# A two-layer kernel whose attention is set up inside the phase before it, and whose first tile's relus all run on one engine

## The reference, cut to what matters

```python
q = jnp.einsum('bnc,ac->bna', X, Wq)          # X is h; a = 64
k = jnp.einsum('bnc,ac->bna', X, Wk)
Vy = jnp.einsum('bnc,dc->bnd', X, Wy_w) + Wy_b
e = jax.nn.relu(_rho_signed_sqrt(q[:, :, None, :] + k[:, None, :, :]))
scores = jnp.einsum('bija,a->bij', e, Wphi)
ex = jnp.exp(scores - jnp.max(scores, axis=-1, keepdims=True))
denom = jnp.sum(ex, axis=-1)
part1 = jnp.einsum('bij,bjc->bic', ex, Vy)
Ew = jnp.einsum('bij,bija->bia', ex, e)
part2 = jnp.einsum('bia,ca->bic', Ew, We_w) + We_b * denom[..., None]
return (part1 + part2) / (denom[..., None] + EPS_DEN)
```

## Time and profile before

| | |
|---|---|
| median of 3 runs | 5102.75 us |
| the profiled execution | 5103.16 us |
| its span, first to last instruction | 5101.5 us |
| busy in the span: PE / DVE / ACT / POOL | 87% / 79% / 67% / 62% |
| phase C's first instruction (SP) to the first root | 1219.28 to 1247.91 us |
| first spread of exponentials in phase C | 1280.37 us |
| last spread | 4377.4 us |

### The profile page before, as it was taken

The page is one execution under the profiler, slowest core; times in us unless marked ns, Lnnn a source line. Parts: engine busy times, 40 slices in busy tenths (PEclk is TensorE's granted clock), DMA queues, the critical chain, the costliest instruction groups (busy, mean ns, idle before and its releaser), DMA issues.

```text
span 5101.5 us, 83954 instructions
## 1 busy us (share of the span) xinstructions
PE 4445.5 (87%) x28586; PEld 2309.7 (45%) x28586; DVE 4020.8 (79%) x6587; ACT 3426.3 (67%) x2401; POOL 3184.0 (62%) x2730
## 2 busy tenths in 40 slices
PE   7888877786889988988988988998898888899998
PEld 4333333464333433433443443443443343577777
DVE  2789895534899999999999999999999999422225
ACT  2232222213999999999999999999988889444343
POOL 0666672433777777777777777777777777243334
PEclk8888887898999999999999999999999999899999
DMA  6000001342000000000000000000000000200002
GB/s 226 0 0 1 0 1 63 116 165 99 1 4 2 2 4 2 17 4 2 2 4 2 17 4 2 2 4 2 11 3 5 2 2 4 100 17 8 16 25 83
DMA packets 70509, 131.01 MB, mean 26 GB/s; under 512 B 8263, under 2 KB 46631, under 8 KB 65888
## 3 DMA queue, kind: packets, MB, share of 16 engines
q1 hardware_dynamic: 61152, 106.21, 6.1%
q0 software_dynamic: 9216, 23.17, 1.2%
HBM read 74.66 MB, written 61.03 MB: 27 GB/s over the span
## 4 chain that ended last, share of the span: by engine, by line
PE 33%; issue 21%; DVE 16%; ACT 13%; POOL 1%; DVEq 1%; DMA 1%; ACTq 0%; POOLq 0%; SPq 0%
PE banks L2206 11%; ACT e_slots L615 10%; PE banks L518 8%; DVE e_slots L858 7%; PE banks L477 7%; DVE e_slots L813 2%; DVE ew L858 1%; PE banks L1641 1%; ACT L632 1%; ACT e_slots L606 1%; PE banks L490 1%; PE banks L292 1%; PE banks L1695 1%; PE banks L1704 1%; PE banks L1592 1%
## 5 line engine op out<-in xcount | busy, mean ns | idle before, releaser
L858 DVE CUSTOM_DVE_ANT_0 e_slots<-e_slots,banks 128x1024 f32<-128x1024 f32 x2048 | 2444.9, 1216 | 120.1 <-PE banks L518 103.6
L615 ACT ACTIVATE e_slots<-e_slots 128x4096 f32<-128x4096 f32 x512 | 1841.1, 3620 | 75.7 <-DVE e_slots L813 51.1
L518 PE MATMUL banks<-ex_parts,sel 128*128 128x512 f32 x4096 | 1521.9, 454 | 169.7 <-DVE ew L858 163.0
L707 POOL TENSOR_SCALAR e_slots<-k,qt 128x1024 f32<-128x1024 f32 x896 | 1002.9, 1121 | 685.7 <-DVE ew L858 644.4
L477 PE MATMUL banks<-e_slots,w_score 128*32 128x256 f32 x16384 | 1260.8, 400 | 172.0 <-ACT e_slots L615 165.5
L518 PEld LDWEIGHTS banks<-ex_parts,sel 128*128 128x128 f32 x4096 | 632.5, 190 | 915.7 <-DVE ew L858 744.0
L713 POOL TENSOR_SCALAR e_slots<-e_slots,qt 128x1024 f32<-128x1024 f32 x896 | 1000.5, 1124 | 64.5 <-POOL e_slots L707 25.7
L477 PEld LDWEIGHTS banks<-e_slots,w_score 128*32 128x32 f32 x16384 | 377.0, 111 | 873.6 <-issue 572.1
L606 ACT ACTIVATE e_slots<-k,qt 128x1024 f32<-128x1024 f32 x512 | 571.3, 1140 | 12.1 <-DVE ew L858 11.9
L2336 POOL TENSOR_TENSOR g_l<-tmp,g_h 128x512 fp32r<-128x512 f32 x192 | 260.4, 1356 | 421.8 <-ACT g_h L2303 288.3
L813 DVE TENSOR_SCALAR e_slots<-k,qt 128x1024 f32<-128x1024 f32 x640 | 466.5, 793 | 0.5 <-POOL qt L717 0.5
(11 more groups left out here) (333 smaller groups left out, 5008.8 us busy)
## 6 DMA issues: line engine op xcount, KB each, us to landing
stage<-in_h SPq DMA_DIRECT2D x16, 1024.0 KB, 4.9
moe_slots<-empty_slot SPq DMA_DIRECT2D x1, 10320.0 KB, 36.3
slots<-moe_slots SPq DMA_DIRECT2D x8, 1290.0 KB, 6.3
moe_out<-empty_slot SPq DMA_DIRECT2D x1, 8192.0 KB, 56.4
two_rows<-moe_out SPq DMA_DIRECT2D x16, 512.0 KB, 5.8
stage<-in_w SPq DMA_DIRECT2D x6, 1024.0 KB, 6.5
x_tokens<-in_x SPq DMA_DIRECT2D x1, 4096.0 KB, 18.6
w_down<-in_w_down SPq DMA_DIRECT2D x1, 4096.0 KB, 12.9
```

Of the source, the lines that this page charges most:

```text
L518: ins = nc.tensor.matmul(spread[n % 2][:, half * W:(half + 1) * W], c_["sel"][:, half, n, :], ex_parts[:, par, :], start=True, stop=True)
L615: nc.scalar.activation(e_slots[:, par, four, :], e_slots[:, par, four, :], ACT.Sqrt, bias=EPS_RHO).then_inc(sqrt_done, 1)
L707: nc.gpsimd.tensor_scalar(e_slots[:, par, n, :], k2[:, :], FLT_MAX, qt[:, par, 1, place(n):place(n) + 1], ALU.min, ALU.max).then_inc(z_cla ...
L858: nc.vector.tensor_tensor_reduce(out=e, in0=e, in1=spread[n % 2], scale=1.0, scalar=0.0, op0=ALU.mult, op1=ALU.add, accum_out=ew[:, q, pla ...
```

## The change

1. **Layout.** `two_rows` is allocated below phase K's buffers, which now lie over the slots and rows of the experts; so phase K's weights (L1490) are loaded after the last of them was read. In phase C, `ex` and `part` are moved next to `e_slots`.
2. **Constants.** The six loads of constants go into phase K, behind the first three fetches of `two_rows`. `row_maps`, `w_score`, `gate_g` and the first keys and queries are made by DVE at the ends of blocks 3, 4, 5 and 6 of phase K (counted from 0), and the masks in block 7; the matmuls by PE after blocks 6 and 7; the casts by ACT after its last copy of keys, in ten instructions instead of four.
3. **First keys, queries, values.** SP loads them after block 5's store; POOL takes the first two tiles' queries at the end of phase K.
4. **First tile.** DVE makes all 16 relus of tile 0. POOL waits for them (`z_v`), counts its own seven as done, makes its slots 0, 1, 4, 5 of tile 1, then tile 0's `parts`, then its slots 7, 8, 9. ACT does the four roots of tile 0 first, then three relus of tile 1 and the exponential.
5. **Scores of tile 1.** PE does the first four after the second spread of tile 0 instead of before tile 0.

Everything from tile 2 on is as before.

```diff
@@ layout
+        b_["two_rows"] = b_base.enter_context(nc.sbuf_tensor("two_rows", [P, 3, TOPK, W // P, C], fp32))
...
-        c_ = phase([("e_slots", [P, 2, NP, T], fp32), ("k2", [P, T], fp32), ("q_pairs", [P, 2, T // 2], fp32),
+        c_ = phase([("e_slots", [P, 2, NP, T], fp32), ("ex", [P, W], fp32), ("part", [P, W], f32r), ("k2", [P, T], fp32), ("q_pairs", [P, 2, T // 2], fp32),
@@ def tile, pe_c
                     ins.then_inc(bc_done, 1)
+                    if first and n == 1:
+                        for of in SCORES_AT.values():
+                            if of[0] == 2:
+                                for m in of[1]:
+                                    scores(t + 1, m, 1)
@@ def act_c
-            first_root(0, 0, None)
-            next_roots(0, 0, None)
-            last_root(0, 0)
-            first_root(1, 1, None)
+            for s in range(PER):
+                sqrt(0, 0, s)
+            for n in (2, 3, 6):
+                relu(1, 1, n, None)
             ex_of(0, 0)
-            next_roots(1, 1, None)
+            relu(1, 1, 10, None)
+            nc.scalar.preload_act_table(ACT.Sqrt)
+            for s in range(3):
+                sqrt(1, 1, s)
@@ def pool_c
-            pool.wait_ge(kq_taken, 1)
-            for par in range(2):
-                tile_queries(par, par)
-            pool.wait_ge(sel_cast, 2 * BPB)
-            for par in range(2):
-                for some in ((0, 1), (4, 5), (7, 8), (9,)):
-                    some_z(par, par, some, None)
+            pool.wait_ge(z_v, Z_BY.count("V"))
+            pool.sem_inc(z_clamped, Z_BY.count("P"))
+            some_z(1, 1, (0, 1), None)
+            some_z(1, 1, (4, 5), None)
             parts(0, 0)
+            some_z(1, 1, (7, 8), None)
+            some_z(1, 1, (9,), None)
@@ def dve_c
-            next_batch(0)
-            dve.wait_ge(sel_cast, 2 * BPB)
-            for t in range(2):
-                for n in range(NP):
-                    z(t, t, n, None)
+            for n in range(NP):
+                nc.vector.tensor_scalar(e_slots[:, 0, n, :], k2[:, :], qt[:, 0, 0, place(n):place(n) + 1], 0.0, ALU.add,
+                                        ALU.max).then_inc({"V": z_v, "A": z_a, "P": z_p}[Z_BY[n]], 1)
+            for n in range(NP):
+                z(1, 1, n, None)
@@ def sp_b
+            sp.wait_ge(turned, NTILES)
             for n, src in (("wk2", "wkT"), ("wq2", "wqT"), ("wy", "wyT"), ("we_k", "weT"), ("bias_k", "bias_c")):
                 sp.dma_start(k_ph[n][:, :, :], a[src]).then_inc(k_loaded, 16)
-            sp.wait_ge(turned, NTILES)
             sp.wait_ge(y_put, NTILES * 16)
             for i in range(3):
                 fetch(i)
+            sp.wait_ge(y_mm_b, NTILES)
+            for to, src in ((c_["we2"][:, :, :], "weT"), (c_["wphi2"][:, :], "wphi"), (k_sel, "k_sel"), (k_selt, "k_selt"),
+                            (c_["ident_c"][:, :], "k_ident"), (k_masks, "k_masks")):
+                sp.dma_start(to, a[src]).then_inc(c_loaded, 16)
...
+                if i == NBLK - 3:
+                    for k in range(2):
+                        sp.wait_ge(k_stored[k], 48)
+                    sp.dma_start(c_["k2_next"][:, :], k_all[:, 0:T]).then_inc(kq_loaded, 16)
+                    sp.dma_start(c_["q_next"][:, :], q_all[:, 0:T // 2]).then_inc(kq_loaded, 16)
+                    sp.dma_start(vy[:, :, 0:C], v_all[:, 0:JT * C].rearrange("p (a c) -> p a c", c=C)).then_inc(vy_loaded, 16)
@@ def pool_b, behind the last store
+            pool.wait_ge(kq_taken, 1)
+            for tl in range(2):
+                nc.gpsimd.tensor_copy(qt[:, tl, :, :], q_pairs[:, :, tl * NP:(tl + 1) * NP]).then_inc(qt_ready, 1)
@@ def pe_b
+                if i == NBLK - 2:
+                    pe.wait_ge(x_moe, NBLK)
+                    pe.wait_ge(c_loaded, 16 * N_C_LOADS)
+                    pe.wait_ge(rows_mapped, 1)
...
+                    nc.tensor.matmul(bank(1), row_maps[:, 2, :], k_sel_at[:, 0:W], start=True, stop=True).then_inc(c_rows, 1)
+            pe.wait_ge(sel_cast, 4)
+            pe.wait_ge(kv_out, NBLK)
+            for n, to in ((1, 0), (2, 6), (3, 7)):
+                ins = nc.tensor.matmul(bank(to), c_["row_maps"][:, 2, :], k_sel_at[:, n * W:(n + 1) * W], start=True, stop=True)
+            ins.then_inc(c_rows, 1)
@@ def dve_b
+            between = {NBLK - 5: row_maps, NBLK - 4: score_weights, NBLK - 3: gates_of_groups, NBLK - 2: first_batch}
...
             for i in range(NBLK):
                 queries(i)
+                if i == NBLK - 1:
+                    row_masks()
...
+                if i in between:
+                    between[i]()
```

More of the change, by code:

```diff
@@ L217, in adaln_kernel @@
                      ("expert", [P, E], fp32), ("out_row", [P, NTT], fp32)] + LN_BUFFERS("b") + LN_BUFFERS("b2"))
-        s_base = ExitStack()
-        b_ |= {n: s_base.enter_context(nc.sbuf_tensor(n, shape, dt)) for n, shape, dt in (
-            ("slots", [P, N_SLOTS, SPP, SLOT_W], fp32), ("hid_t", [P, 3, HC, P], fp32),
-            ("y_rows", [P, E * SPP, C], fp32), ("weight", [P, E, SPP], fp32), ("goes_to", [P, E, SPP], u32),
-            ("first", [P, SPP], fp32), ("second", [P, SPP], fp32), ("w_first", [P, SPP], fp32),
-            ("w_second", [P, SPP], fp32))}
@@ L230, in adaln_kernel @@
-        s_base.close()
-        b_ |= phase([("two_rows", [P, 3, TOPK, W // P, C], fp32)])
+        b_ |= phase([("slots", [P, N_SLOTS, SPP, SLOT_W], fp32), ("hid_t", [P, 3, HC, P], fp32),
+                     ("y_rows", [P, E * SPP, C], fp32), ("weight", [P, E, SPP], fp32), ("goes_to", [P, E, SPP], u32),
+                     ("first", [P, SPP], fp32), ("second", [P, SPP], fp32), ("w_first", [P, SPP], fp32),
+                     ("w_second", [P, SPP], fp32)])
+        b_["two_rows"] = b_base.enter_context(nc.sbuf_tensor("two_rows", [P, 3, TOPK, W // P, C], fp32))
@@ L508, in turned_back, with tile @@
                 ins.then_inc(out_mm, 1)
-            def tile(t, q, last=False, sums_of=None, values=None, more_sums_of=None, turn=None):
+            def tile(t, q, first=False, last=False, sums_of=None, values=None, more_sums_of=None, turn=None):
                 par = q % 2
@@ L560, in group_on @@
             def group_on(tg, values, last=False):
-                tile(tg * GT + 2, 2, last)
-                tile(tg * GT + 3, 3, last, tg, values)
+                tile(tg * GT + 2, 2, last=last)
+                tile(tg * GT + 3, 3, last=last, sums_of=tg, values=values)
                 sums_of_e(tg)
@@ L574, in pe_c @@
                 scores(0, m, 0)
-            for n in range(NP):
-                if n in SCORES_AT and SCORES_AT[n][0] == 2:
-                    for m in SCORES_AT[n][1]:
-                        scores(1, m, 1)
-            tile(0, 0)
+            tile(0, 0, first=True)
             tile(1, 1)
@@ L590, in act_c @@
             act.wait_ge(c_loaded, 16 * N_C_LOADS)
[L591 to L598 removed]
+            act.wait_ge(sel_cast, N_SEL)
             def relu(t, par, n, freed):
@@ L793, in next_batch @@
             def next_batch(b):
[L795 to L800 removed]
+                dve.wait_ge(z_a, b * (NTI * Z_BY.count("A")))
+                dve.wait_ge(z_v, b * (NTI * Z_BY.count("V")))
+                dve.wait_ge(z_p, b * (NTI * Z_BY.count("P")))
+                dve.wait_ge(qt_ready, b * NTI)
                 dve.wait_ge(kq_loaded, b * 32 + 32)
@@ new lines, in score_weights @@
+            def score_weights():
+                own.link(nc.vector.memset(c_["w_score"][:, :, :, :], 0.0))
+                for s in range(PER):
+                    for i in range(2):
+                        rows = slice(i * A, (i + 1) * A)
+                        for half in range(BPB):
+                            at = HALF_ROWS * half + 2 * s + i
+                            ins = nc.vector.tensor_copy(c_["w_score"][rows, s, half, at:at + COPY_ROWS + 1:COPY_ROWS],
+                                                        c_["wphi2"][rows, 0:1].broadcast_to([A, 2]))
+                own.link(ins)
@@ new lines, in gates_of_groups, with first_batch @@
+            def gates_of_groups():
+                for c in range(CC):
+                    ins = nc.vector.tensor_copy(c_["gate_g"][:, c, :, :], mod[1][:, 2 * GA + c, :].unsqueeze(2).broadcast_to(
+                        [P, B, NG]))
+                own.link(ins)
+                nc.vector.memset(vy[:, :, C:C + 1], 1.0).then_inc(c_cast, 1)
+            def first_batch():
+                dve.wait_ge(kq_loaded, 32)
+                nc.vector.tensor_copy(k2[:, :], c_["k2_next"][:, :])
+                nc.vector.tensor_copy(q_pairs[:, 0, :], c_["q_next"][:, :])
+                nc.vector.tensor_scalar(q_pairs[:, 1, :], c_["q_next"][:, :], -1.0, None, ALU.mult).then_inc(kq_taken, 1)
```

114 lines of the change are left out of this document (45 added, 69 removed).

## The result

The changed kernel took 5061.8 us (median of 5050.4, 5061.4, 5062.2 and 5073.0) against 5102.2 for the kernel before: a ratio of 0.992, 95% interval 0.990 to 0.995. Later, in longer comparisons on two chips, it took 5054.7 against 5101.0 (0.990, 0.989 to 0.992) and 5053.6 against 5102.0 (0.991, 0.989 to 0.992). The direction was as forecast. The size was not: 30.8 us were promised, and 40 to 48 came. The forecast of 5072 missed by 10 us, and its range (from 5067) lies above the median.

What follows compares the result with a forecast made beforehand. Phase K was taken as bound by PE, the start of phase C by an uncovered chain of set-up and waits. 21.8 + 9.7 - 0.7 = 30.8 us off 5103.16 gives 5072.4, as median 5072.0; range 5067 to 5080.

Steps and rivals of the forecast that it cites:

- Start of phase C (21.8): Set-up between phase K and the first relu goes into phase K, so the first relu starts 21.8 us earlier.
- rivals 1 to 3: Constants' traffic delays phase K, 5078, 0.12; relus slow without POOL, 5081, 0.07; set-up time only moved, 5093 to 5103, 0.05.
- First two tiles (9.7): Phase C, first relu to tile 1's last root: 39.6 us instead of 49.3, so 9.7 saved.
- Start of phase K (0.7 lost): Weights loaded later slow the scattered rows that release the fetch: 0.7 us lost, bounds 0 and 3.5.
- The rule on the shared ports: DVE and POOL relus exclude each other: DVE's five of tile 1 at 1.87 us each, gain 29.4 instead of 30.8.
- After it 126 tiles follow in a loop, which a shift does not change: After tile 1's roots both kernels keep the same order, so the end moves by what that instant moves.
- the constant 31 us that I named as a sign: From tile 1's last root on, a constant distance of some 31 us to the kernel before would show the forecast right.
- Rival 4: `ex` and `part` elsewhere in SBUF make each phase C tile dearer; at 0.26 us more, 5105; chance 0.04.
- turned by 1097: Sign of being right: phase K's first `two_rows` turned by 1097 us from the start.
- a fetch after 1089: Sign that the constants' traffic reaches phase K's path: a fetch issued after 1089 us; chance 0.12.

Runs made afterwards that it cites:

- before_plus_11: The kernel before with 11 small VectorE memsets added at the start of phase C, in its wait: 5092.9 us against 5110.2.
- before_plus_128: The kernel before with 128 small VectorE memsets added at the start of phase C, in its wait: 5107.5 us against 5110.2.
- after_filled: The changed kernel with the second position's spread matmuls issued three times in three of four tiles: 5048.9 us, against 5101.0 for the kernel before.
- after_filled_2: The same kernel as after_filled, run again in the third series: 5054.1 us, against 5053.6 for the unaltered changed kernel and 5102.0 for the kernel before.

## Why the prediction was right and wrong

**Start of phase C (21.8): right.** 122.4 to 123.9 us in the seven traces with the set-up moved, 143.1 to 145.5 in the seven without; the medians, 123.8 and 145.1, lie 21.3 apart. What takes 1.4 to 2 us off in four of the fourteen, no run shows. The steps inside hold too. POOL's drain ends the phase, ACT's casts are done before that, at 1212.9, and the first relu comes right behind the drain, at 1215.1. Of the losses that rivals 1 to 3 named none is there: the fetch comes no later (below), 16 relus took 10.7 us and not 23.2, and the casts did not end the phase.

**First two tiles (9.7): right as an interval.** 39.5 us against 39.6 forecast. The terms in it erred and cancelled: the 16 relus took 0.67 each and not 0.75, 10.7 in all; the exponential started at 21.5 (22.0 forecast) and the first spread at 25.1 (25.2). By the fourth tile's exponential 1.1 us of it was lost again.

**Start of phase K (0.7 lost): not there.** The term stood for scattered rows that land later and hold up the fetch. From the issue of the last of them to the fetch it was 1088.00 - 1085.53 = 2.47 us before and 1083.40 - 1080.97 = 2.43 after. The term was mis-sized by its whole 0.7. With the weights issued late, PE waits 2.03 us for `bias_k`, off the path:

```profile
1081.70 0.61 PE L1610 MATMUL banks<-ones,we_k 128*128 128x1 f32 x4 [2.03 <-DMA bias_k<-in_bias_c]
```

**The rule on the shared ports.** In this execution VectorE's five relus took 3.40 us, 0.68 each, as if alone, while POOL's pair beside them took 4.99 instead of 2.22. That is as the Trainium skill says (SBUF — State Buffer, "SBUF: two separate sides"): whichever instruction starts first has the pair of ports for its whole length, and the other one fully blocks. In the earlier trace rows ten relus took 14.48 us and both sides were slow. I had forecast mutual slowing for this place, and for who is slowed the rule was the better one; but what I worked out from it, 1.87 us for each relu of VectorE, was as wrong. Why VectorE keeps the ports through five relus here, and shares them there, no run shows. The last root came at 39.5 all the same, where the forecast had 39.6.

**"After it 126 tiles follow in a loop, which a shift does not change": wrong.** This step failed, and it carries the miss. A shift in time indeed changed nothing. A shift in instruction places did, and my part-by-part list had the 11 added relus as time on VectorE only. The order of VectorE's instructions would have shown the shift, and the waits of before had the row of six idles. I never asked what "issue" was in a loop that was otherwise the same in all passes. That is worth 16 to 17 us (16.4 in the traces, 17.2 by before_plus_11): 21.8 + 9.7 + 17.2 = 48.7, against 48.4 and 46.3 in the long comparisons and 40.4 in the first one, which had only four runs of each kernel. Nor was the distance from tile 1 on the constant 31 us that I named as a sign: it grew in the last batch's loop.

**Slips that cost nothing.** Rival 4's tile, (4377.4 - 1280.37) / 128 = 24.2 us, divides by 128 where 127 tiles lie between the two spreads; it is 24.4. And the signs given as times from the start (turned by 1097, a fetch after 1089) can't be read, because the start of phase K moves by 18 us between executions; only the intervals can.

**The rule that would have warned me.** The Trainium skill has it (Runtime: NRT & Kernel Launch, "Instruction fetch mechanics"): instruction memory holds two blocks, is filled sequentially, and a taken branch whose target isn't in it stalls for a fetch of the target's block. The idles behind the branch agree with that in part: VectorE stands still for code, but it was the second packet behind the branch that it waited for, and with 64 memsets it refetched and did not stall. The Trainium skill's figure, blocks of 16 KiB or 256 instructions, does not fit VectorE here. That would be 64 bytes an instruction; q14's packets carry 8.2 KB, so 128 instructions at that size, and the place repeated after 128 (by 256, before_plus_128 would have moved the loop by half a block). The measurement decides.

**The spread between runs.** The first turned rows of phase K came anywhere from 1091.4 to 1109.2 us in the fourteen profiled executions, and the unchanged kernel's runs in one series lay 27 us apart. The two profiled executions of the filled kernel lie 15.8 us apart, of which 14.7 had arisen before these rows. That is probably why 5050 to 5073 was seen in four runs; what makes the part before phase K vary, no run shows. No single run here measures less than 10 us.

**Why 2.1 us in one set of kernels and 0.9 in the other.** The places say it. At 0 and 128 the idle is about 2.1, and it begins right at the end of the relus. At 1 and 2 places back one multiply-reduce of 1.21 us still runs, and 2.1 - 1.2 = 0.9. The end of the idle is the same in both, 5.1 to 5.6 us behind the branch's own record.

**What stays open.** How many of the 128 places are bad. For the last batch's loop 0, 128 and those 1 and 2 back are, and 9, 11 and 64 further are not. Also open is why a pass fetches 5 packets, when 286 instructions at 128 a packet are 2.2.

## What to carry to other kernels

An edit moves all code behind it on its engine. If a loop with a long body follows, compare the instruction queues' packets and the "issue" rows of the two traces before crediting the difference to the edit. Look in any tuned loop for idles behind issue right after the branch back: a handful of instructions in an idle place ahead of the loop may remove them (here 11, 17 us), and an edit that removes instructions may bring them back. Count the semaphore instructions too: they take places like any other.

## What the runs showed of the hardware

- VectorE's loop of 286 instructions refetched 5 packets of 8.2 KB per pass at some places and none at others, and a shift by 128 instructions changed nothing. At the bad places VectorE stood idle for 2.1 or 0.9 us near the loop's head and went on 1.25 to 1.53 us behind the landing of the second packet. With 64 instructions more, other loops refetched as much and no idle was seen.
- Keeping PE busy in its wait (1.45 us more of matmuls in three of four tiles) kept the granted clock at 2.4 GHz through 30 groups in after_filled and through all but one fall in after_filled_2, where it fell 22 times in after. The loop in the profiled executions became 8 to 14 us shorter, but no median showed it clearly.
- Five relus of VectorE ran at 0.68 us each beside GpSimd, whose pair took 4.99 us instead of 2.22; ten others beside GpSimd took 1.45 each.
